# Orders of work in three graph layers and at the ends of attention, and rounded passes in layer 1

## What is computed

```python
x = x + attention(layernorm(x), adj)        # 8 heads, masked by adj, relu at the end
x = x + lstm(layernorm(x))                  # 256 steps over the nodes
x = x + graph_layers(layernorm(x), adj)     # 3 layers, below
x = x + quantised_product(layernorm(x))     # fp8 grid, 256 x 256 weight

for l in range(3):                          # graph_layers
    scores = leaky(si[:, :, None] + sj[:, None, :] + attn_b[l])   # si, sj = x @ halves of attn_w[l]
    agg = softmax(where(mask, scores, -inf)) @ x
    h = layernorm(x + agg) * g1 + beta1
    x = layernorm(h + gelu(h @ W1 + b1) @ W2 + b2) * g2 + beta2
```

## Time and profile before

| | us |
|---|---|
| median of 3 runs (range) | 2994.3 (2993.64 to 2996.24) |
| the profiled execution, its time | 2992.49 |
| its span | 2990.7 |
| attention | 0 to about 612 |
| LSTM | about 612 to 1277 |
| graph layers | about 1280 to 2873 |
| last phase | about 2873 to 2991 |
| TensorE, VectorE, ScalarE, GpSimd busy | 90%, 69%, 62%, 54% of the span |

### The profile page before, as it was taken

The page is one execution under the profiler, slowest core; times in us unless marked ns, Lnnn a source line. Parts: engine busy times, 40 slices in busy tenths (PEclk is TensorE's granted clock), DMA queues, the critical chain, the costliest instruction groups (busy, mean ns, idle before and its releaser), DMA issues. The chain is left out here.

```text
span 2990.7 us, 116485 instructions
## 1 busy us (share of the span) xinstructions
PE 2683.2 (90%) x44066; PEld 2435.4 (81%) x44224; DVE 2052.4 (69%) x6005; ACT 1839.8 (62%) x4930; POOL 1620.6 (54%) x2681
## 2 busy tenths in 40 slices
PE   6999999978888888859999999999999999999957
PEld 5777777767777777749999999899899999999956
DVE  6887888734444444446777776888888888888768
ACT  4666666644444444437777776777777677777734
POOL 6777777510000000037777765666666677788744
PEclk9999999989999999969999999999999999999979
DMA  3111111000000000020000011100000100000002
GB/s 92 40 35 35 35 41 38 13 10 13 12 13 12 13 13 13 13 76 25 26 23 25 26 44 31 27 7 9 9 7 9 45 9 9 9 7 9 8 25 91
DMA packets 110836, 74.59 MB, mean 25 GB/s; under 512 B 51504, under 2 KB 109360, under 8 KB 110512
## 3 DMA queue, kind: packets, MB, share of 16 engines
q1 hardware_dynamic: 96800, 61.03, 7.1%
q10 hardware_dynamic: 13968, 12.72, 1.4%
HBM read 51.68 MB, written 22.02 MB: 25 GB/s over the span
## 5 line engine op out<-in xcount | busy, mean ns | idle before, releaser
L1560 PE MATMUL g_H<-g_hT_upper,g_w_upper 128*128 128x256 f32 x1536 | 453.9, 295 | 0.0
L1560 PE MATMUL g_H<-g_hT_rest,g_w_upper 128*128 128x256 f32 x1536 | 436.0, 284 | 0.0
L1560 PE MATMUL g_H<-g_hT_upper,g_w_rest 128*128 128x256 f32 x1536 | 435.7, 284 | 0.0
L745 POOL COPY l_xt<-seq 128x64 f32 x256 | 60.6, 237 | 598.2 <-PE l_O L756 596.5
L1159 ACT ACTIVATE g_act_raw<-g_H,g_small 128x256 f32<-128x256 f32 x768 | 303.3, 469 | 22.2 <-PE g_H L1560 21.0
L329 ACT ACTIVATE a_probs<-a_S,a_nmax 128x256 f32<-128x256 f32 x512 | 236.7, 480 | 121.6 <-DVE a_nmax L422 88.9
L1051 POOL TENSOR_TENSOR g_h<-g_r,g_g_row 128x256 f32<-128x256 f32 x192 | 138.1, 741 | 294.7 <-DVE g_r L1360 294.0
L1560 PEld LDWEIGHTS g_H<-g_hT_rest,g_w_upper 128*128 128x128 f32 x1536 | 295.7, 193 | 2.5
L1560 PEld LDWEIGHTS g_H<-g_hT_upper,g_w_upper 128*128 128x128 f32 x1536 | 295.4, 192 | 2.7 <-DVE g_hT_rest L1308 0.2
L1587 PE MATMUL g_F<-g_w_upper,g_act_upper 128*128 128x256 f32 x1024 | 293.1, 286 | 4.5 <-DVE g_act_rest L1346 4.1
L1560 PEld LDWEIGHTS g_H<-g_hT_upper,g_w_rest 128*128 128x128 f32 x1536 | 295.8, 193 | 0.0
...
## 6 DMA issues: line engine op xcount, KB each, us to landing
...
hidden<-l_hs SPq DMA_DIRECT2D x512, 16.0 KB, 1.4
...
```

The source lines that it names most:

```text
L745: pool.tensor_copy(xt[i][:, :, :], t.seq[:, :, s * 2 + i, :]).then_inc(xt_done, 1)
L1560: last = pe.matmul(hidden_bank[m // 2][:, m % 2 * N:(m % 2 + 1) * N], w[:, c, m * P:(m + 1) * P], x[:, c, :], start=(c == 0 and k == 0), s ...
```

## The change

Attention: the fourth weight's arrival is counted with the rows, and VectorE splits the weights before it handles rows and graph 1. At the end, `split_bias` runs ahead of the last `spread_out`, the halving of LSTM weights ahead of the last `rden_out`; the last two normalisations go from GpSimd to VectorE; graph 30 is turned through `in_bank`, and the projection of graph 31 no longer waits for it.

Graph layers: turned rows go to `agg_bank` and the shifted bias to `turn_bank`; `turn_probs` drops its wait on `hT_done`. `up` of chunks 0 and 1 comes ahead of `turn_probs` and `scores`. `attend` is cut into `warm_up` (table load and tiny record), ahead of `hT_out`, and the exponentials, behind it. In layer 1, `down` of banks 1 to 3 becomes three rounded passes, bank 0 stays plain and runs between the halves of `up`; ScalarE makes the upper part of banks 1 and 3. W1 and W2 are split in halves, W1's upper part on ScalarE. `next_pair` is cut into two halves around `split_hT`. VectorE starts a graph with `feed(behind)` and its statistics. Graphs enter straight into `t.nodes` without the buffer `hs`, and the entry's order changes on all engines. The last phase's weight is loaded from within the graph phase into `t.aw`.

The diff, cut to its core (indentation shortened; lines that only follow from a new count or name are left out):

```diff
@@ -179,8 +179,9 @@
-    for w, src in ((wq, a["L0_gnn_Wq"]), (wk, a["L0_gnn_Wk"]), (wv, a["L0_gnn_Wv"]), (wo, a["L0_gnn_Wo"])):
-        sp.dma_start(w[:, :, :], src.rearrange("(c p) n -> p c n", p=P)).then_inc(weights_in, 16)
+    for w, src, done in ((wq, a["L0_gnn_Wq"], weights_in), (wk, a["L0_gnn_Wk"], weights_in),
+                         (wv, a["L0_gnn_Wv"], weights_in), (wo, a["L0_gnn_Wo"], rows_in)):
+        sp.dma_start(w[:, :, :], src.rearrange("(c p) n -> p c n", p=P)).then_inc(done, 16)
@@ -308,11 +310,10 @@
+    split_bias()
...
-        norm2(b)
-    split_bias()
@@ -367,13 +369,13 @@
-    rden_out(B - 1)
-    for b in range(B - 2, B):
-        xn2T_out(b)
...
+    rden_out(B - 1)
+    for b in range(B - 2, B):
+        xn2T_out(b)
@@ -462,6 +464,15 @@
+    def norm2(b):
...
+        dve.wait_ge(heads_ps, B)
+        alone(dve, rstd2_done, b + 1, passed)
+        for it in range(NT):
+            last = dve.tensor_scalar(xn2[:, it, :], t.x[:, b, it, :], mv2[:, it, 0:1], rstd2[:, it, :],
+                                     ALU.subtract, ALU.mult)
+        last.then_inc(xn2_done, 1)
@@ -494,11 +505,7 @@
-    dve.wait_ge(rows_in, 4 * 16)
-    dve.memset(qscale[:, :], HD ** -0.5)
-    dve.tensor_scalar(bqs_col[:, :], bq_col[:, :], HD ** -0.5, None, ALU.mult).then_inc(bqs_done, 1)
-    moments1(1)
-    dve.wait_ge(weights_in, 4 * 16)
+    dve.wait_ge(weights_in, 3 * 16)
@@ -507,15 +514,21 @@
+    dve.wait_ge(rows_in, 5 * 16)
+    dve.memset(qscale[:, :], HD ** -0.5)
+    dve.tensor_scalar(bqs_col[:, :], bq_col[:, :], HD ** -0.5, None, ALU.mult).then_inc(bqs_done, 1)
+    moments1(1)
...
+    norm2(B - 2)
...
+    norm2(B - 1)
@@ -534,6 +547,10 @@
+        if isinstance(b, int) and b == B - 2:
+            pe.wait_ge(rden_done, B)
+            turn(in_bank, xn2).then_inc(xn2T_ps, 1)
+            return
@@ -628,7 +645,7 @@
-        after(pe, xn2T_done, b)
+        after(pe, xn2T_done, b if not isinstance(b, int) or b < B - 1 else B - 2)
@@ -917,24 +935,21 @@
-        ON_ACT = ((), (1, 3), (3,))
...
+        ON_ACT = ((1, 3), (1, 3), (3,))
+        FIRST = (1, 0, 0)
@@ -1006,13 +1020,17 @@
...
-            with sp.Fori(4, B) as e:
-                load_hidden(e)
+            load_hidden(4, hs_in)
+            with sp.Fori(5, B) as e:
+                sp.wait_ge(extra_x, e)
+                load_hidden(e, hs_in)
+    sp.wait_ge(pair_done, 2 * (L - 1) * B)
+    sp.dma_start(t.aw[:, :, :], a["L1_ffn_weight"].rearrange("(c p) n -> p c n", p=P)).then_inc(t.ffn_weight_in, 16)
@@ -1077,8 +1095,11 @@
-        pool.wait_ge(hs_in, e * 16 + 16)
-        pool.tensor_tensor(t.x[:, e, :, :], t.x[:, e, :, :], hs[:, :, :], ALU.add).then_inc(extra_x, 1)
+        if isinstance(e, int) and e < 4:
+            pool.wait_ge(hs_first[e], 16)
+        else:
+            pool.wait_ge(hs_in, e * 16 - 48)
+        pool.tensor_tensor(t.x[:, e, :, :], t.x[:, e, :, :], t.nodes[:, e, :, :], ALU.add).then_inc(extra_x, 1)
@@ -1088,10 +1109,14 @@
-        for e in range(4):
+        for e in range(2):
...
+        enter(2)
...
+        rsqrt_extra(2)
+        enter(3)
+        rsqrt_extra(3)
@@ -1191,33 +1218,49 @@
+    def w1_uppers(l, half):
...
+        act.wait_ge(w1_in, (l + 1) * 16)
+        act.wait_ge(cols_in, (l + 1) * COLS_IN)
+        after(act, hidden_ps, l * B * NB)
+        part = slice(half * FF // 2, (half + 1) * FF // 2)
+        for c in range(KC):
+            last = act.activation(w1_upper[:, c, part], w1_of(l)[:, c, part], ACT.Copy, scale=g1_col[:, c:c + 1])
+        last.then_inc(w1_upper_done, 1)
...
-        act.activation(hT_upper[:, :, :], turn_bank[:, :], ACT.Copy).then_inc(hT_upper_done, 1)
+        act.activation(hT_upper[:, :, :], agg_bank[:, :], ACT.Copy).then_inc(hT_upper_done, 1)
...
-        for e in range(2):
-            norm_extra(e, e)
+        norm_extra(0, 0)
...
+        warm_up(*at)
...
+        norm_extra(1, 1)
+        w1_uppers(0, 0)
+        w1_uppers(0, 1)
+        slope(*soon)
+        load_mask(*soon)
+        norm1(*at)
+        warm_up(*soon)
...
-        norm1(*at)
...
-        slope(*soon)
...
-        load_mask(*soon)
...
+        crossing = ahead and now[0] < ahead[0]
+        feed(*now, range(0, 1))
...
-        feed(*now, range(0, 2))
+        feed(*now, range(1, 2))
@@ -1225,12 +1268,18 @@
+        if crossing:
+            w1_uppers(ahead[0], 0)
...
-            attend(*soon)
+            warm_up(*soon)
...
+        if crossing:
+            w1_uppers(ahead[0], 1)
+        if soon:
+            attend(*soon)
@@ -1305,31 +1354,26 @@
-        dve.tensor_tensor(hT_rest[:, :, :], turn_bank[:, :].rearrange("p (c n) -> p c n", c=KC),
+        dve.tensor_tensor(hT_rest[:, :, :], agg_bank[:, :].rearrange("p (c n) -> p c n", c=KC),
...
-    def split_w1(l):
-        dve.wait_ge(w1_in, (l + 1) * 16)
-        dve.wait_ge(cols_in, (l + 1) * COLS_IN)
-        after(dve, hidden_ps, l * B * NB)
+    def split_w1(l, half):
+        dve.wait_ge(w1_upper_done, 2 * l + half + 1)
+        part = slice(half * FF // 2, (half + 1) * FF // 2)
...
-            last = dve.tensor_scalar(w1_upper[:, c, :], w1_of(l)[:, c, :], g1_col[:, c:c + 1], None, ALU.mult)
-        last.then_inc(w1_upper_done, 1)
-        dve.wait_ge(w1_upper_done, l + 1)
-        for c in range(KC):
-            last = dve.scalar_tensor_tensor(out=w1_rest[:, c, :], in0=w1_of(l)[:, c, :], scalar=g1_col[:, c:c + 1],
-                                            in1=w1_upper[:, c, :].bitcast(F32), op0=ALU.mult, op1=ALU.subtract)
+            last = dve.scalar_tensor_tensor(out=w1_rest[:, c, part], in0=w1_of(l)[:, c, part],
+                                            scalar=g1_col[:, c:c + 1], in1=w1_upper[:, c, part].bitcast(F32),
+                                            op0=ALU.mult, op1=ALU.subtract)
...
-    def split_w2(l):
...
-        for half, loaded in enumerate((w2_half_in, net_in)):
-            dve.wait_ge(loaded, (l + 1) * 16)
-            part = slice(half * MC // 2, (half + 1) * MC // 2)
-            dve.tensor_copy(w2_upper[:, part, :], w2_raw[:, part, :]).then_inc(w2_upper_done, 1)
-            dve.wait_ge(w2_upper_done, (l - 1) * 2 + half + 1)
-            dve.tensor_tensor(w2_rest[:, part, :], w2_raw[:, part, :], w2_upper[:, part, :].bitcast(F32),
-                              ALU.subtract).then_inc(w2_done, 1)
+    def split_w2(l, half):
...
+        dve.wait_ge((w2_half_in, net_in)[half], (l + 1) * 16)
+        part = slice(max(half * MC // 2, 2 * FIRST[l]), (half + 1) * MC // 2)
+        dve.tensor_copy(w2_upper[:, part, :], w2_raw[:, part, :]).then_inc(w2_upper_done, 1)
+        dve.wait_ge(w2_upper_done, 2 * l + half + 1)
+        dve.tensor_tensor(w2_rest[:, part, :], w2_raw[:, part, :], w2_upper[:, part, :].bitcast(F32),
+                          ALU.subtract).then_inc(w2_done, 1)
@@ -1412,67 +1456,77 @@
+        moments_extra(0, 0)
...
-        moments_extra(0, 0)
...
-        split_w1(0)
...
+        reciprocals(*at)
+        turned(*at)
...
-        reciprocals(*at)
...
-        turned(*at)
+        split_w1(0, 0)
+        aggregated(*at)
...
-        aggregated(*at)
+        largest(*soon)
+        split_w1(0, 1)
...
+        shift_bias(0)
+        split_hT(*at)
...
-        split_hT(*at)
-        largest(*soon)
...
-        shift_bias(0)
...
+        l, b = now
...
-        crossing = ahead and now[0] < ahead[0]
+        crossing = ahead and l < ahead[0]
+        first = isinstance(b, int) and b == 0
+        pairing = past and gone is None
+        if behind:
+            feed(*behind)
+            stats2_of(*behind)
...
-            feed(*behind)
+            moments2(*behind)
+        if first:
+            split_w2(l, 0)
+        if FIRST[l] == 0:
+            split_act(l, b, range(0, 1))
...
-        if behind:
-            stats2_of(*behind)
-            moments2(*behind)
...
-        if in_parts(now[0]):
-            if isinstance(now[1], int) and now[1] == 0:
-                split_w2(now[0])
-            split_act(*now, range(0, 1))
-        if ahead:
...
-        if in_parts(now[0]):
-            split_act(*now, range(1, NB))
+        split_act(l, b, range(1, 2))
+        if first:
+            split_w2(l, 1)
+        split_act(l, b, range(2, 3))
...
+        split_act(l, b, range(3, NB))
...
-            split_w1(ahead[0])
+            split_w1(ahead[0], 0)
...
-        if past and gone is None and not crossing:
-            next_pair(*past)
+        if pairing and not crossing:
+            next_pair(*past, 0)
...
+            split_w1(ahead[0], 1)
...
-            next_pair(*past)
+            if pairing:
+                next_pair(*past, 0)
+        if pairing:
+            next_pair(*past, 1)
@@ -1507,7 +1561,8 @@
-        after(pe, hT_done, n)
+        if isinstance(b, int) and b == 1:
+            pe.wait_ge(bias_done, l + 1)
@@ -1531,17 +1584,17 @@
-                last = pe.transpose(turn_bank[:, c * N + it * P:c * N + (it + 1) * P],
```

(21 more changed lines are left out.)

93 lines of the change are left out of this document (47 added, 46 removed).

## The result

The changed kernel takes 3006.1 us (median of six runs, 3002.8 to 3010.3), the kernel before 2996.1 beside it (2993.6 to 2999.7): ratio 1.0033, 95% interval 1.0021 to 1.0046. That is slower, by more than the 0.2% that can be told from no change. The profiled execution took 3003.4 us with a span of 3001.6, so 10.9 more than the 2992.5 of before; the two traces are compared on that.

What follows compares the result with a forecast made beforehand. The prediction took TensorE to bound layer 1, and its waits on the split, behind ScalarE, to lengthen layers 2 and 3. Terms summed to -11.8 from 2992.5, so 2980.7, 2982.5 as median; likeliest range 2955 to 3003, wide range 2930 to 3006.

Steps and rivals of the forecast that it cites:

- the likeliest case: Whole kernel: VectorE bounds layer 1 at 17.2 to 18.6 us a graph; 2982 us, range 2955 to 3003; chance 0.50.
- Layer 1: Graph at 18.0 us (bounds 16.5 and 18.6): +54 over 26 graphs, +1 for the last four.
- The list without meetings: VectorE's in-order work in a layer-1 graph, without GpSimd collisions, ends at 16.5 us; bank 2's gelu ends at 9.9.
- Rival B: Layer 1: VectorE finds room, 15.9 to 16.5 us a graph, +54 becomes 0 to +15, time 2928 to 2943; chance 0.25.
- ScalarE's chain: Layer 1: from the fourth bank at 10.5 through gelu, copy, scaling, warm-up, `hT_out` and split, graph ends at 15.85 us.
- rival D: Layer 1: rounding works, TensorE bounds a graph at 15.05 us, -23 instead of +54, time 2905; chance 0.04.
- Layer 2: Exponentials moved behind `hT_out`: a graph from 16.01 to 15.0 us, -29 over 29 graphs (bounds -36 and -10).
- Layer 3: Same cover on ScalarE, VectorE late as well: 0.5 us a graph, -14.5 over 29 graphs (bounds -7 and -19).
- Layer changes: Layer changes and halved W1, W2 together: -1.5 us (bounds -6 and +4).
- Attention: Start: queries at 13.5 instead of 17.59, -4.1 us; end: LSTM begins at about 604.7 instead of 612.2, -7.5 us.
- Entry: Start of graph phase: TensorE's first full graph at 1313.3 against 1323.4; -8 us (bounds -11 and -4).
- Last phase: Waiting of 2.30 us on the weight goes: -2.2 us (bounds -2.3 and 0, if GpSimd's reduction starts no earlier).

## Why the prediction was wrong

The forecast was -11.8 and it came to +10.9. The median of 3006.1 lies 3 us above the range of the likeliest case. That case had the right mechanism (VectorE bounds layer 1 in an in-order wait and in meetings with GpSimd), with its largest term sized too small, and that turned the sign.

- **Layer 1: +55 forecast, +78 measured. This is the step that failed.** I took 18.0 us for the graph; it is 18.76 on average. The list without meetings, 16.5, was right: bank 2 starts 10.05 into the graph where I had 9.9. The meetings cost 2.0 (dot products 1.67, subtraction 0.35), the top of my 1.35 to 2.0, where I had taken 1.5. That is 0.4 a graph, 11 us. The clock's 0.35 a graph, 9 us, was not in the sum at all: I priced TensorE's new idle time as time alone, not as clock. Its bound of 18.6 was passed for that reason. The remaining 3 us lie in the layer's first two graphs (17.7 and 19.8, with W2's split among them) and at the change to layer 2 (21.5 for 20.5).
- **What the list said but I didn't draw from it.** The wait and the meetings depend on the order: one swap, the dot products ahead of bank 2, takes 2.7 us off a graph. Rival B, "VectorE finds room", was wrong for the changed kernel. Its times (2928 to 2943) are those of the kernel with the swap: VectorE does not find room by itself, but it was one swap away.
- **ScalarE's chain**, 15.85, was right. In the graphs that both enter others and pair it is not the pace; even with the swap VectorE is, at 16.07. In the layer's last graphs, which enter none, it is: the changed kernel takes 16.00 and 15.87 there. ScalarE goes from bank 3's gelu to `hT_out` without a pause, and VectorE's split waits for it:

```profile
1867.03 1.28 ACT L1165 ACT_TABLE_LOAD   x1
1868.33 0.21 ACT L1165 ACTIVATE g_small<-eps_power 128x2 f32<-128x2 f32 x1
1868.44 0.58 ACT L1236 ACTIVATE g_hT_upper<-g_A 128x512 fp32r<-128x512 f32 x1
```

```profile
1869.05 0.69 DVE L1357 TENSOR_TENSOR g_hT_rest<-g_A,g_hT_upper 128x512 fp32r<-128x512 f32 x1 [0.29 <-ACT g_hT_upper L1236]
```

- **TensorE's own price** was right: rival D's 15.05 is what the last graphs with three rounded banks show (14.8 to 15.2). But two chains stand before it, VectorE's list and the 1.58 us from the turned rows to `up`.
- **Layer 2: -29 forecast, -25.4 measured** with the change of layer in it; period 15.17 for 15.0. **Layer 3: -14.5 and -14.3**, right, though a third of its 0.52 a graph is not the exponentials' place, as their return showed. `hT_out` stands behind the warm-up as described, the remaining wait is 0.20. ScalarE, then TensorE:

```profile
2105.56 0.21 ACT L1165 ACTIVATE g_small<-eps_power 128x2 f32<-128x2 f32 x1
2105.67 0.58 ACT L1236 ACTIVATE g_hT_upper<-g_A 128x512 fp32r<-128x512 f32 x1
```

```profile
2107.11 0.38 PE L1613 MATMUL g_H<-g_hT_upper,g_w_upper 128*128 128x256 f32 x1 [0.20 <-DVE g_hT_rest L1357]
```

- **Layer changes: -1.5 forecast, about 0.** The two graphs at each change take 39.6 and 37.8 us, before 39.2 and 38.2.
- **Attention: -11.6 forecast, -11.4 between the two traces.** That it agrees so closely is luck twice over. The other twelve traces with this attention phase have the LSTM's first record at 601.5 to 606.2 and not at 600.8; tried alone, the phase gives 12.4 between medians, 8 to 18 in the interval, so the term is confirmed in size but not to a microsecond. And the parts missed in opposite directions: the start gave 2.5, not 4.1 (queries at 15.06, in the other traces 14.1 to 15.2; the casts wait for the weights until 10.37, a microsecond later than I had them), the end 8.9, not 7.5, as the projection ran at the full clock (1.99 us instead of 3.75), a case that I had as the bound.
- **Entry: -8 forecast, -15.2 measured**, beside 0.9 that the LSTM phase itself took less. One part that the sum left out is `shift_bias`. Before, it stood between the first turned rows (1315.79) and `turn_probs`, with 6.83 us at a granted clock of 0.50. Now it comes ahead of the turned rows, right behind other work and at a granted clock of 0.97 at first, takes 4.61, and ends at 1293.77, when the scaled rows are just there (1293.44). How much of the 7.2 that makes was not tried alone and stays open. In the forecast's favour this miss hid a third of layer 1's.
- **Last phase: -2.2 forecast, 0 measured**, the bound that I had named. GpSimd's reduction starts no earlier, 5.8 us into the phase in both kernels, and the weight had come before that. From the changed kernel:

```profile
2884.73 0.10 POOL L1743 MEMSET q_zero<- 128x1 f32 x1 [2.13 <-POOLq L978]
2890.56 0.37 POOL L1745 PARTITION_ALL_REDUCE q_tops<-q_most  x1 [5.73 <-issue]
```

The Trainium skill, GPSIMD Engine Reference, "2.1 Instruction dispatch", says that the first call of a freshly loaded GpSimd kernel pays about 6 us that no instruction shows. The 5.73 agrees with it, and by that rule alone the term would have been 0.

The rule of the Trainium skill that the prediction weighed for layer 1 (SBUF — State Buffer, "Who interferes with whom") had given 18.5 a graph, nearer to the 18.41 without the clock than my 18.0. Its kind is confirmed once more for operations with two inputs: the subtraction and the dot products each grow by 0.4 to 0.6 us. A whole record of GpSimd of 0.72 was never added. The operation on two columns grows by 0.53 too, but it reads one tensor, so that sentence on two inputs doesn't cover it.

The Trainium skill's rule on a drain behind the table load (ScalarE: Activation LUTs, "What ACT_TABLE_LOAD costs") was rightly set aside: the record behind layer 2's load at 2104.27 begins at 2105.56, 1.29 later.
